# Order of the second layer's matmuls in the first feed-forward, and signals for the first constants of the next stage

## The chip, the cores and the metric

One core of a Trainium2 chip runs the whole program. The metric is the device time of one execution in microseconds (us). The engines are TensorE (PE in profile rows, its weight loads PEld), VectorE (DVE), ScalarE (ACT), GpSimd (POOL) and SyncE (SP), which here issues every transfer. Each engine runs its own list of instructions in order and meets the others through semaphores.

## The reference, cut to what matters

Two transformer layers work on 2048 tokens of width 512. Each layer adds an attention and a feed-forward, both fed by the same normalised input. The change touches the feed-forward of layer 0 and the start of the projections of layer 1:

```python
# layer 0, feed-forward: 16 blocks of 128 hidden units, 4 chosen for each token
h = jnp.einsum('nf,ibf->nib', xf, W1b)                      # first layer
h = jax.nn.gelu(h, approximate=False) * mask[:, :, None]
y = jnp.einsum('nib,fib->nf', h, W2b)                       # second layer
...
x = x + _L0_attn_ref(...) + _L0_ffn_ref(...)
xn = _layernorm(x, axis=-1)                                 # start of layer 1
k_r = hidden_states @ kr_w.T                                # hidden_states is xn
c_kv = hidden_states @ down_w.T
k_c = c_kv @ upk_w.T
v = c_kv @ upv_w.T
k = k * cos + _rotate_half(k) * sin
```

## The kernel before, in words

All products are made in three matmuls: each float32 operand is split into a high part and a low remainder, and `split_matmul` (L47 to L52) adds high by high, high by low and low by high into one bank of PSUM. A matmul with 512 moving columns is the unit of everything below.

`feed_forward0` goes through the 16 hidden blocks in four quarters (`NQ`), of four blocks each (`BPQ`). Within a quarter it goes through four chunks of 512 tokens (`NCH`), each of four tiles of 128 tokens (`TPC`). So there are 16 iterations. In one iteration:

- TensorE makes the first layer, 4 blocks of 12 matmuls, each into its bank `HB[b]`, and signals `hid`. Then it makes the second layer, another 48 matmuls, into the four banks `YB[t]`, one for each token tile.
- ScalarE takes a block through Gelu (`f_gl`, L919), and after the masking rounds it to the high part (`f_hT_hi`, L923). It makes the Gelu of block b before the high part of block b-1.
- VectorE multiplies the block by its mask (`f_h`, L1013, signal `masked`).
- GpSimd subtracts to make the low part (`f_hT_lo`, L940, signal `h_lo`). Only after `h_lo` may TensorE use the block in the second layer.
- VectorE adds the four finished `YB[t]` to the running sum `xacc` (L1025, signals `y_done` and `y_added`).
- Beside this, VectorE unpacks the 4-bit weights of layer 1's feed-forward, 21 operations in an iteration of quarters 1 and 2 and of the first three iterations of quarter 3 (L969 to L988), and splits the next quarter's weights in quarters 0 to 2 (ScalarE L905, VectorE L951).

The second layer is issued in two halves. The first waits for blocks 0 and 1 and makes, tile by tile, their six matmuls; the second waits for blocks 2 and 3 and does the same. `y_done` comes tile by tile in the second half.

`projections1` follows behind a barrier of all engines. SyncE issues the transfers: two weights, six constants (identity, epsilon and four rotation tables), two more weights, the first piece of the query weights, and the store of `xacc`. All six constants count on one signal, `c_in`. Meanwhile VectorE makes the statistics of the first 512 tokens (L1281, L1285); ScalarE takes the square root (L1232, needs epsilon), VectorE normalises (L1289, L1294), TensorE transposes (L1366, needs the identity), ScalarE and VectorE split the four weights (L1246, L1313) and the transposed chunk (L1237, L1300), and TensorE starts the key product (L50 to L52 on `k_wk`). The rotation tables are first used when VectorE multiplies that product (`k_rp`, L1325). ScalarE and TensorE each wait for the whole of `c_in` at the start of their list.

Of the kernel before, what the change touches and what calls it, by code (L numbers as in the profile page):

```python
# [14 lines left out]
P = 128  # L15
# [31 lines left out]
def split_matmul(pe, out, lhs, rhs, first, last, lsel, rsel):  # L47

    (lh, ll), (rh, rl) = lhs, rhs
    pe.matmul(out, lh[lsel], rh[rsel], start=first, stop=False)  # L50
    pe.matmul(out, lh[lsel], rl[rsel], start=False, stop=False)  # L51
    return pe.matmul(out, ll[lsel], rh[rsel], start=False, stop=last)  # L52
# [674 lines left out]
def feed_forward0(nc, ps, d, xacc):  # L727
# [3 lines left out]
    BPQ = NB // NQ  # L731
# [4 lines left out]
    with ExitStack() as ctx:  # L736
# [8 lines left out]
        w2 = [sb(f"w2_{s}", [P, 2, BPQ, C], F32R) for s in ("hi", "lo")]  # L745
# [4 lines left out]
        hT = [sb(f"hT_{s}", [P, BPQ, CH], F32R) for s in ("hi", "lo")]  # L750
# [40 lines left out]
        with nc.Block() as block:  # L791
# [235 lines left out]
            @block.tensor  # L1027
            def _(pe):
                for q in range(NQ):
                    p = q % 2  # L1030
                    with pe.Fori(0, NCH) as c:
                        it = c + q * NCH
                        if q == 0:
                            pe.wait_ge(xt_in.sem, xt_in.now(c, 32))

                        pe.wait_ge(w_lo.sem, (q + 1) * PRO if q else KC)
                        for b in range(BPQ):
                            pe.wait_ge(gelu.sem, gelu.before(it, b + 1))
                            for k in range(KC):
                                last = split_matmul(pe, HB[b], [w[:, p] for w in w1], xt, k == 0, k == KC - 1,  # L1040
                                                    np.s_[:, k, b * P:(b + 1) * P],
                                                    (slice(None), k, bass.ds(c * CH, CH)))
                            last.then_inc(hid.sem, 1)
                        if q == 0:
                            pe.wait_ge(w_lo.sem, PRO)
                        for bs in (range(BPQ - 2), range(BPQ - 2, BPQ)):
                            pe.wait_ge(h_lo.sem, h_lo.now(it, bs[-1] + 1))
                            for t in range(TPC):
                                if bs[0] == 0:
                                    pe.wait_ge(y_added.sem, y_added.before(it, t + 1))  # L1050
                                for b in bs:
                                    last = split_matmul(pe, YB[t], hT, [w[:, p] for w in w2], b == 0, b == BPQ - 1,
                                                        np.s_[:, b, t * P:(t + 1) * P], np.s_[:, b, :])
                                if bs[0] > 0:
                                    last.then_inc(y_done.sem, 1)


# [8 lines left out]
def projections1(nc, ps, d, xacc, xt):  # L1066

    with ExitStack() as ctx:
# [3 lines left out]
        def sig(name, per, credit=False):  # L1072
            return Signal(nc, ctx, "k1_" + name, per, credit)
# [28 lines left out]
        BANKS = [*XB, *MB]  # L1102

        apart = sig("apart", 0)
        c_in = sig("c_in", 0)
        w_in = [sig(f"w_in{i}", 0) for i in range(len(weights))]
        w_hi = sig("w_hi", 0)
        w_lo = sig("w_lo", 0)
# [23 lines left out]
        q_sum = sig("q_sum", 2 * NCH, credit=True)  # L1132
        q_stored = [sig(f"q_stored{i}", 32 * NCH // 2, credit=True) for i in range(2)]

        CONSTS = [(ident[:], d["c_ident"]), (eps[:], d["c_eps"]), (cosk[:], d["c_cosk"]), (sink[:], d["c_sink"]),
                  (cosq[:], d["c_cosq"]), (sinq[:], d["c_sinq"])]
        ALL_CONSTS = 16 * len(CONSTS)

        def staged(n):

            _, k, m = weights[n][0].shape
            room = (kq[:].rearrange("p t n -> p (t n)"), qo[:].rearrange("p a b n -> p (a b n)"))[n // 2]
            return room[:, (n % 2) * KC * R1:(n % 2) * KC * R1 + k * m].rearrange("p (k n) -> p k n", k=k)
# [4 lines left out]
        with nc.Block() as block:  # L1148
            @block.sync
            def _(sp):  # L1150
                for s in q_stored:
                    s.give_credit(sp)
                for n, name in enumerate(names[:2]):
                    sp.dma_start(staged(n), d[name].rearrange("(k p) n -> p k n", p=P)).then_inc(w_in[n].sem, 16)
                for dst, src in CONSTS:
                    sp.dma_start(dst, src).then_inc(c_in.sem, 16)
                for n, name in enumerate(names[2:], 2):
                    sp.dma_start(staged(n), d[name].rearrange("(k p) n -> p k n", p=P)).then_inc(w_in[n].sem, 16)

                def load_wq(g):  # L1160
                    sp.dma_start(wq_stage[:], d["WqT"][:, bass.ds(g * QW, QW)].rearrange("(k p) n -> p k n", p=P)
                                 ).then_inc(wq_in.sem, 16)

                load_wq(0)
                sp.dma_start(d["x2"], xacc[:]).then_inc(x_stored.sem, 16)
                for c in range(NCH):
                    sp.wait_ge(xt_lo.sem, xt_lo.now(c, KC))
                    for s in range(2):
                        sp.dma_start(d["xt"][s][:, :, c * CH:(c + 1) * CH],
                                     xt[s][:, :, c * CH:(c + 1) * CH].bitcast(F32)).then_inc(x_stored.sem, 16)  # L1170
                    for t, ready in ((0, rotated.now(c, 1)), (2, rotated.now(c, 2))):
                        sp.wait_ge(rotated.sem, ready)
                        sp.dma_start(d["KT"][t, :, c * CH:(c + 1) * CH], kq[:, t, :]).then_inc(k_stored.sem, 16)
                    for t, ready in ((1, kc_out.now(c, 1)), (3, kc_out.now(c, 2))):
                        sp.wait_ge(kc_out.sem, ready)
                        sp.dma_start(d["KT"][t, :, c * CH:(c + 1) * CH], kq[:, t, :]).then_inc(k_stored.sem, 16)
                    for t in range(TPC):
                        sp.wait_ge(v_out.sem, v_out.now(c, t + 1))
                        seq, tile = divmod(c * TPC + t, SEQ // P)
                        for r in range(4):  # L1180
                            sp.dma_start(d["V"].rearrange("g b p j e -> b j p g e")[seq, 4 * tile + r, :, :, :],
                                         vt[32 * r:32 * r + 32, t % 2, :].rearrange("p (g e) -> p g e", e=HD1)
                                         ).then_inc(v_stored[t % 2].sem, 16)

                def store_q(g, c):
                    for i in range(2):
                        sp.wait_ge(q_sum.sem, q_sum.now(g, 2 * c + i + 1))
                        sp.dma_start(d["QT"][bass.ds(g, 1), i, :, c * CH:(c + 1) * CH].squeeze(0), qo[:, c % 2, i, :]
                                     ).then_inc(q_stored[c % 2].sem, 16)

                with sp.Fori(0, NKV - 1) as g:
                    sp.wait_ge(wq_lo.sem, wq_lo.now(g, 1))
                    load_wq(g + 1)
                    for c in range(NCH):
                        store_q(g, c)
                for c in range(NCH):
                    store_q(NKV - 1, c)
                sp.wait_ge(x_stored.sem, 16 + 32 * NCH)
                sp.wait_ge(k_stored.sem, k_stored.now(NCH, 0))
                for s in v_stored:  # L1200
                    sp.wait_ge(s.sem, s.now(NCH, 0))
                for s in q_stored:
                    sp.wait_ge(s.sem, s.now(NKV, 0))
# [21 lines left out]

            @block.scalar
            def _(act):
                act.wait_ge(c_in.sem, ALL_CONSTS)

                def root(c):  # L1230
                    act.wait_ge(ln_chain.sem, ln_chain.now(c, 2 * TPC))
# [44 lines left out]
            def _(dve):  # L1276
# [20 lines left out]
                def split_turned(c):  # L1297
                    for k in range(KC):
                        dve.wait_ge(xt_hi.sem, xt_hi.now(c, k + 1))
                        nc.vector.tensor_tensor(xt[1][:, k, c * CH:(c + 1) * CH], XB[k],  # L1300
                                                xt[0][:, k, c * CH:(c + 1) * CH].bitcast(F32), ALU.subtract
                                                ).then_inc(xt_lo.sem, 1)
# [8 lines left out]
                for n, w in enumerate(weights):  # L1311
                    dve.wait_ge(w_hi.sem, n + 1)
                    nc.vector.tensor_tensor(w[1][:], staged(n), w[0][:].bitcast(F32), ALU.subtract  # L1313
                                            ).then_inc(w_lo.sem, 1)
                dve.wait_ge(c_in.sem, ALL_CONSTS)
                split_turned(0)
                for c in range(NCH):
                    if c + 1 < NCH:
                        dve.wait_ge(ln_chain.sem, ln_chain.now(c + 1, 0))
# [35 lines left out]
            @block.tensor  # L1355
            def _(pe):
                q_done.give_credit(pe)
                pe.wait_ge(c_in.sem, ALL_CONSTS)

                def turn(c):  # L1360
                    pe.wait_ge(ln_chain.sem, ln_chain.now(c + 1, 0))
# [851 lines left out]
```

## Time and profile before

| what | us |
|---|---|
| median of three runs (2312.14 to 2317.91) | 2313.44 |
| the profiled execution: its time | 2313.69 |
| its span, first to last instruction | 2311.9 |
| TensorE busy in the span | 2077.5 |
| VectorE busy | 1544.6 |
| ScalarE busy | 874.0 |
| GpSimd busy | 486.2 |
| the first feed-forward's matmuls, first to last start | 324.30 to 684.53 |
| first transposes of the projections | 700.60 |
| first matmul of the key product | 706.91 |

A timeline row reads: start, duration, engine, line, operation, what it writes and reads, count. What stands in brackets at its end is the idle time of the engine before it and who ended it. Matmuls overlap: a row's duration is its latency, and the distance of two starts is what one costs. A row of a stage gives, for each engine, busy time and number of instructions, then the granted TensorE clock as a share of full speed, the share of the transfer engines and GB/s.

### The profile page before, as it was taken

The numbers are of one execution on the slowest core, as the hardware profiler recorded it, in microseconds if no ns is written. First come the engines' busy times: TensorE is split into PE (matmuls) and PEld (weight loads), VectorE is DVE, ScalarE is ACT, GpSimd is POOL, SyncE is SP. The second block draws the span as 40 slices with busy tenths as digits, with TensorE's granted clock in tenths as the row PEclk, the third lists the DMA queues.
The fourth block names the chain that finished last, engine by engine and source line by source line (L and its number), as shares of the span: only waits on it lengthen the run. The fifth ranks groups of instructions, "written<-read, shape, count | busy, mean of one in ns | idle before, by whom it ended". The sixth has DMA issues, their size and how long they took to land. (4 is left out here: it accounts for less than half of the span.)

```text
span 2311.9 us, 54178 instructions
## 1 busy us (share of the span) xinstructions
PE 2077.5 (90%) x22192; PEld 1468.3 (64%) x22192; DVE 1544.6 (67%) x2534; ACT 874.0 (38%) x1836; POOL 486.2 (21%) x408
## 2 busy tenths in 40 slices
PE   7999969999988999778888888888888699999997
PEld 5777758877766788634444444444444588787776
DVE  6544423799966354478989988889998330477776
ACT  4222123222213200045655655565665221234443
POOL 0111112222310145401111111111111444221111
PEclk9999989999998999979999999999999899999999
DMA  5122154344326533333443333343332555320101
GB/s 179 56 93 75 38 195 151 109 134 132 121 94 250 177 121 121 110 77 84 102 106 99 93 100 87 84 113 107 92 92 77 214 170 183 111 90 19 55 1 37
DMA packets 197121, 251.26 MB, mean 109 GB/s; under 512 B 38496, under 2 KB 119712, under 8 KB 194208
## 3 DMA queue, kind: packets, MB, share of 16 engines
q1 hardware_dynamic: 196032, 247.85, 34.7%
q8 instruction: 166, 2.72, 0.5%
q14 instruction: 59, 0.48, 0.1%
q10 hardware_dynamic: 864, 0.21, 0.0%
HBM read 165.08 MB, written 82.90 MB: 107 GB/s over the span
## 5 line engine op out<-in xcount | busy, mean ns | idle before, releaser
L1614 ACT ACTIVATE a_prob<-ps,a_nmax 128x256 f32<-128x256 f32 (+7 forms) x512 | 377.4, 739 | 349.4 <-DVE a_nmax L1642 211.2
L1727 PE MATMUL ps<-a_kt,a_q 64*128 64x512 f32 (+5 forms) x1536 | 380.4, 536 | 85.3 <-ACT a_prob L1614 63.6
L1642 DVE TENSOR_REDUCE a_nmax<-ps 128x1 f32<-128x1024 f32 (+3 forms) x256 | 256.1, 1000 | 73.0 <-PE ps L1727 71.5
L1659 DVE STREAM_TRANSPOSE a_pt_long<-a_prob 128x512 f32<-128x512 f32 (+3 forms) x512 | 278.1, 580 | 0.0
L1727 PEld LDWEIGHTS ps<-a_kt,a_q 64*128 64x128 f32 x1536 | 143.1, 193 | 184.5 <-ACT a_prob L1614 116.7
L1741 PE MATMUL ps<-a_pt_long,a_v 32*64 32x256 f32 (+3 forms) x7808 | 228.6, 344 | 2.5 <-issue 1.0
L2021 DVE SCALAR_TENSOR_TENSOR f_part<-ps,f_gu_scale,f_part 128x512 f32<-128x512 f32 x264 | 184.6, 745 | 65.8 <-PE ps L2068 52.5
L1741 PEld LDWEIGHTS ps<-a_pt_long,a_v 32*64 32x64 f32 x7808 | 153.9, 132 | 105.1 <-issue 77.1
L1694 POOL TENSOR_TENSOR a_o<-a_left 128x256 f32<-128x256 f32 x128 | 90.3, 726 | 595.5 <-ACT a_left L1624 595.5
L940 POOL TENSOR_TENSOR f_hT_lo<-f_h,f_hT_hi 128x512 fp32r<-128x512 f32 x64 | 89.7, 1407 | 294.5 <-ACT f_hT_hi L923 294.5
L1724 PE MATMUL ps<-a_causal,a_identb 64*128 64x128 bf16 x1024 | 112.2, 224 | 39.5 <-ACT a_prob L1614 39.5
L1645 DVE TENSOR_REDUCE a_nmax<-ps 128x2 f32<-128x1024 f32 (+3 forms) x128 | 104.8, 819 | 37.7 <-PE ps L1727 37.3
L919 ACT ACTIVATE f_gl<-ps 128x512 f32<-128x512 f32 x64 | 38.3, 599 | 225.0 <-PE ps L52 225.0
L50 PE MATMUL ps<-f_xt_hi,f_w_hi 128*128 x256 | 100.4, 392 | 17.8 <-DMA f_xt_lo<-scratch_xt 17.8
L50 PE MATMUL ps<-o_wo_hi,o_oT_hi 128*128 128x512 f32 x256 | 100.4, 392 | 15.8 <-POOL o_oT_lo L1844 15.8
L1659 DVE STREAM_TRANSPOSE a_pt_short<-a_prob 128x512 f32<-128x512 f32 (+3 forms) x256 | 114.2, 484 | 0.0
L1724 PEld LDWEIGHTS ps<-a_causal,a_identb 64*128 64x128 bf16 x1024 | 45.7, 95 | 104.8 <-issue 78.1
L2010 POOL TENSOR_TENSOR f_hT_lo<-f_h,f_hT_hi 128x512 fp32r<-128x512 f32 x44 | 57.5, 1306 | 254.9 <-ACT f_hT_hi L1966 254.9
L1223 POOL TENSOR_TENSOR k_qo<-k_rp 128x512 f32<-128x512 f32 x64 | 87.4, 1387 | 102.5 <-DVE k_rp L1346 102.5
L1741 PEld LDWEIGHTS ps<-a_pt_short,a_v 32*64 32x64 f32 x3712 | 65.9, 132 | 67.5 <-issue 67.4
L50 PE MATMUL ps<-f_w_hi,f_hT_hi 128*128 128x512 f32 x256 | 101.3, 396 | 6.4 <-POOL f_hT_lo L940 6.4
L1346 DVE TENSOR_TENSOR k_rp<-ps,k_cosq 128x512 f32<-128x512 f32 x64 | 43.9, 685 | 94.1 <-POOL k_qo L1223 81.2
(228 smaller groups left out, 4552.4 us busy)
## 6 DMA issues: line engine op xcount, KB each, us to landing
a_q<-scratch_QT SPq DMA_DIRECT2D x512, 64.0 KB, 2.1
scratch_QT<-k_qo SPq DMA_DIRECT2D x64, 256.0 KB, 2.3
a_v<-scratch_V SPq DMA_DIRECT2D x64, 256.0 KB, 4.3
scratch_OT<-a_o SPq DMA_DIRECT2D x32, 512.0 KB, 3.4
o_of<-scratch_OT SPq DMA_DIRECT2D x32, 512.0 KB, 4.1
f_block<-in_packed SPq DMA_DIRECT2D x33, 256.0 KB, 3.4
f_mask<-scratch_maskT SPq DMA_DIRECT2D x16, 512.0 KB, 5.1
a_kt<-scratch_KT SPq DMA_DIRECT2D x128, 64.0 KB, 4.2
```

Source lines behind the costliest of these rows:

```text
L50: pe.matmul(out, lh[lsel], rh[rsel], start=first, stop=False)
L940: nc.gpsimd.tensor_tensor(hT[1][:, b, :], h[:, b % 2, :], hT[0][:, b, :].bitcast(F32), ALU.subtract).then_inc(h_lo.sem, 1)
L1223: nc.gpsimd.tensor_tensor(qo[:, c % 2, i, :], rp[:, 2 * i, :], rp[:, 2 * i + 1, :], op).then_inc(q_sum.sem, 1)
L1614: last = nc.scalar.activation(prob[:, n % PRING, s].rearrange("p (a w) -> p a w", w=w), SC[n % 2][:, a, 0:w], ACT.Exp, bias=nmax[:, n % 4, ...
L1642: nc.vector.tensor_reduce(nmax[:, n % 4, 0:1], SC[n % 2][:, :, 0:width(0, t)], AX.XY, ALU.max, negate=True).then_inc(maxed, 1)
L1645: nc.vector.tensor_reduce(nmax[:, n % 4, :], SC[n % 2][:, :, 0:width(1, t)], AX.X, ALU.max, negate=True).then_inc(maxed, 1)
L1659: last = nc.vector.transpose(pt[hf][:, lo:hi, h, t - FIRST[hf], :], src.rearrange("p (j k) -> p j k", k=32))
L1694: nc.gpsimd.tensor_tensor(o[:, :, :, i, :], left[:, i, 0], left[:, i, 1], ALU.mult).then_inc(o_done, 1)
L1724: pe.matmul(sc[:, a, w - P:w], identb[r, s, :], causal[r, s, :], start=s == 0, stop=False, skip_group_check=True)
L1727: last = pe.matmul(sc[:, a, 0:w], q[r, slot, heads[a * hf], :], kt[r, b, keys], start=not masked, stop=True, skip_group_check=True)
L1741: last = pe.matmul(out[:, :, a - t0:4, :], v[rows, b, j, :], pt[hf][rows, j, c::2, a - t0:4, :], start=j == 0, stop=j == BLOCKS[hf] - 1, s ...
L2021: nc.vector.scalar_tensor_tensor(part[:, s % 2, i, :], PB[(2 * k + i) % 4], gu_scale[:, s % NBK, i, k:k + 1], part[:, s % 2, i, :], ALU.mu ...
```

## The change

The second layer of the first feed-forward is issued in four parts instead of two: one block at a time, over all four token tiles, each part behind its own wait for `h_lo`. The matmuls and their number are the same. In the projections, epsilon and the identity get a signal of their own, `first_in`, and are issued first; the four weights follow, and the four rotation tables come behind them. ScalarE and TensorE wait for `first_in` alone. VectorE waits for the tables after it has split the first transposed chunk.

```diff
-                        for bs in (range(BPQ - 2), range(BPQ - 2, BPQ)):
-                            pe.wait_ge(h_lo.sem, h_lo.now(it, bs[-1] + 1))
+                        for b in range(BPQ):
+                            pe.wait_ge(h_lo.sem, h_lo.now(it, b + 1))
                             for t in range(TPC):
-                                if bs[0] == 0:
+                                if b == 0:
                                     pe.wait_ge(y_added.sem, y_added.before(it, t + 1))
-                                for b in bs:
-                                    last = split_matmul(pe, YB[t], hT, [w[:, p] for w in w2], b == 0, b == BPQ - 1,
-                                                        np.s_[:, b, t * P:(t + 1) * P], np.s_[:, b, :])
-                                if bs[0] > 0:
+                                last = split_matmul(pe, YB[t], hT, [w[:, p] for w in w2], b == 0, b == BPQ - 1,
+                                                    np.s_[:, b, t * P:(t + 1) * P], np.s_[:, b, :])
+                                if b == BPQ - 1:
                                     last.then_inc(y_done.sem, 1)
...
-        c_in = sig("c_in", 0)
+        first_in, c_in = sig("first_in", 0), sig("c_in", 0)
...
-        CONSTS = [(ident[:], d["c_ident"]), (eps[:], d["c_eps"]), (cosk[:], d["c_cosk"]), (sink[:], d["c_sink"]),
-                  (cosq[:], d["c_cosq"]), (sinq[:], d["c_sinq"])]
+        CONSTS = [(cosk[:], d["c_cosk"]), (sink[:], d["c_sink"]), (cosq[:], d["c_cosq"]), (sinq[:], d["c_sinq"])]
...
-                for n, name in enumerate(names[:2]):
+                sp.dma_start(eps[:], d["c_eps"]).then_inc(first_in.sem, 16)
+                sp.dma_start(ident[:], d["c_ident"]).then_inc(first_in.sem, 16)
+                for n, name in enumerate(names):
                     sp.dma_start(staged(n), d[name].rearrange("(k p) n -> p k n", p=P)).then_inc(w_in[n].sem, 16)
                 for dst, src in CONSTS:
                     sp.dma_start(dst, src).then_inc(c_in.sem, 16)
-                for n, name in enumerate(names[2:], 2):
-                    sp.dma_start(staged(n), d[name].rearrange("(k p) n -> p k n", p=P)).then_inc(w_in[n].sem, 16)
...
             def _(act):
-                act.wait_ge(c_in.sem, ALL_CONSTS)
+                act.wait_ge(first_in.sem, 32)
...
             def _(dve):
...
+                split_turned(0)
                 dve.wait_ge(c_in.sem, ALL_CONSTS)
-                split_turned(0)
...
             def _(pe):
                 q_done.give_credit(pe)
-                pe.wait_ge(c_in.sem, ALL_CONSTS)
+                pe.wait_ge(first_in.sem, 32)
```

## Rows read from the trace of the kernel before

**Rows 1.** Busy time by engine in seven iterations of quarters 1 and 2.
```profile
436.00:596.00 160.00, 154.49 (x674) 125.65 (x674) 145.66 (x217) 40.78 (x70) 40.49 (x28) 1.00 0.43 132
```

**Rows 2.** Timeline of TensorE where the second layer starts, quarters 0 and 3.
```profile
402.65 0.39 PE L52 MATMUL ps<-f_xt_hi,f_w_lo 128*128 x1
403.03 0.47 PE L50 MATMUL ps<-f_w_hi,f_hT_hi 128*128 128x512 f32 x1
...
606.38 0.39 PE L51 MATMUL ps<-f_xt_lo,f_w_hi 128*128 x1
606.61 0.39 PE L52 MATMUL ps<-f_xt_hi,f_w_lo 128*128 x1
607.86 0.50 PE L50 MATMUL ps<-f_w_hi,f_hT_hi 128*128 128x512 f32 x1 [0.86 <-POOL f_hT_lo L940]
```

**Rows 3.** Waits of VectorE in the same 160 us: total, times, longest.
```profile
DVE f_w_lo L951 <- ACT f_w_hi L905: 9.5, 7, 1.4
```

**Rows 4.** Timeline of VectorE: first maskings of two iterations, and two unpacking steps.
```profile
601.87 0.68 DVE L1013 TENSOR_TENSOR f_h<-f_gl,f_mask 128x512 f32<-128x512 f32 x1
...
606.60 1.76 DVE L980 SCALAR_TENSOR_TENSOR f_block<-f_mag,f_block 128x512 f32<-128x512 f32 x1
608.39 1.68 DVE L982 TENSOR_TENSOR f_block<-f_block,f_sign 128x512 int32<-128x512 int32 x1
...
622.59 0.68 DVE L1013 TENSOR_TENSOR f_h<-f_gl,f_mask 128x512 f32<-128x512 f32 x1
```

**Rows 5.** Timeline of GpSimd: low part of block 1, then of blocks 1, 2 and 3.
```profile
401.55 1.38 POOL L940 TENSOR_TENSOR f_hT_lo<-f_h,f_hT_hi 128x512 fp32r<-128x512 f32 x1 [1.43 <-ACT f_hT_hi L923]
...
606.03 1.78 POOL L940 TENSOR_TENSOR f_hT_lo<-f_h,f_hT_hi 128x512 fp32r<-128x512 f32 x1 [1.30 <-ACT f_hT_hi L923]
608.23 1.29 POOL L940 TENSOR_TENSOR f_hT_lo<-f_h,f_hT_hi 128x512 fp32r<-128x512 f32 x1 [0.43 <-ACT f_hT_hi L923]
611.42 1.32 POOL L940 TENSOR_TENSOR f_hT_lo<-f_h,f_hT_hi 128x512 fp32r<-128x512 f32 x1 [1.90 <-ACT f_hT_hi L923]
```

**Rows 6.** Timeline where two of GpSimd's subtractions stand back to back.
```profile
653.13 3.10 POOL L940 TENSOR_TENSOR f_hT_lo<-f_h,f_hT_hi 128x512 fp32r<-128x512 f32 x2 [1.35 <-ACT f_hT_hi L923]
...
653.57 1.52 DVE L969 TENSOR_SCALAR f_sign<-f_block,f_up_shift 128x512 int32<-128x512 int32 x1
```

**Rows 7.** Timeline of VectorE at the start of the projections.
```profile
698.32 0.18 DVE L1289 RECIPROCAL k_rstd<-k_std 128x4 f32<-128x4 f32 x1 [9.46 <-ACT k_std L1232]
...
714.02 0.69 DVE L1325 TENSOR_TENSOR k_rp<-ps,k_cosk 128x512 f32<-128x512 f32 x1 [4.47 <-PE ps L52]
```

**Rows 8.** Timeline of ScalarE at the start of the projections.
```profile
688.95 1.28 ACT L1232 ACT_TABLE_LOAD   x1 [13.03 <-DVE k_mv L1285]
697.99 0.30 ACT L1232 ACTIVATE k_std<-k_mv,k_eps 128x4 f32<-128x4 f32 x1 [7.76 <-DMA k_sinq<-in_c_sinq]
...
700.62 1.04 ACT L1246 ACTIVATE k_wuv_hi<-k_qo 128x1024 fp32r<-128x1024 f32 x1
```

**Rows 9.** Timeline of TensorE: the start of the key product.
```profile
706.91 0.80 PE L50 MATMUL ps<-xt_hi,k_wk_hi 128*128 128x512 f32 x1 [2.66 <-DVE xt_lo L1300]
```

**Rows 10.** Transfers issued between 680 and 800 us: count, KB, issue to landing.
```profile
scratch_V<-k_vt SPq DMA_DIRECT2D x64, 64.0 KB, 1.9
...
k_cosk<-in_c_cosk SPq DMA_DIRECT2D x1, 512.0 KB, 6.0
...
k_qo<-in_wuvT SPq DMA_DIRECT2D x1, 512.0 KB, 9.6
...
k_eps<-in_c_eps SPq DMA_DIRECT2D x1, 0.5 KB, 4.6
```

**Rows 11.** Timeline of SyncE: first, fifth and tenth transfer of the projections.
```profile
686.07 0.39 SPq L1154 DMA_DIRECT2D k_kq<-in_wkT  x1
...
688.07 0.43 SPq L1156 DMA_DIRECT2D k_cosk<-in_c_cosk  x1
...
690.45 0.96 SPq L1158 DMA_DIRECT2D k_qo<-in_wuvT  x1
```

## The prediction

> **What bounds the kernel now.** I read the busy time by stage first, then the waits of each engine in the stage that the change touches, then the timelines at the points of the waits.
>
> The second and third quarters of the feed-forward hold two engines near their limit: in seven iterations (160 us) TensorE is busy 154.5 us and VectorE 145.7 us [rows 1]. The question is which one waits for the other. In those 160 us VectorE has one kind of wait only, for the high part of the split weights, 9.5 us in seven pieces of 1.4 us [rows 3]. That wait hangs on its own last masking and not on TensorE. Busy time and this wait make 155.2 of the 160 us; the rest is small gaps between dependent unpacking steps. So VectorE never waits for a matmul there: it is the bound, at 160/7 = 22.9 us for an iteration. TensorE needs less. Its starts are 0.227 us apart (606.38 and 606.61 [rows 2]), so 96 matmuls take 21.8 us, and the rest is a stall at the start of each second layer: 607.86 - 606.61 - 0.23 = 1.02 us [rows 2], released by the low part of block 1, ready at 606.03 + 1.78 = 607.81 [rows 4 and 5]. There are eight such stalls, one in each of eight iterations (447.33 is the first, 607.86 the last).
>
> Where VectorE has room (quarter 0, the first iteration of quarter 1, and quarter 3 behind its first iteration), TensorE is the bound. Even there the second layer starts late: 403.03 against 402.65 + 0.23 = 402.88 [rows 2]. The low part of block 1 is ready only at 401.55 + 1.38 = 402.93 [rows 5]. The matmul behind it starts 0.31 us later instead of 0.23.
>
> Between the last matmul of the feed-forward (684.53) and the key product (706.91 [rows 9]) TensorE does only 16 transposes. The chain there runs: square root, normalising, weight splits, transposed chunk, key product. The square root starts at 697.99, released by the last rotation table [rows 8], though it needs none of them; its table load began at 688.95, when the statistics were done, and ended at 690.23 [rows 8].
>
> **The feed-forward's part.** Let S be the start of the second layer. Before, it needs block 1 at S and block 3 at S + 24 x 0.227 = S + 5.44. After, blocks 0, 1, 2, 3 are needed at S, S + 2.72, S + 5.44, S + 8.16. No need comes earlier. The instructions are the same; two more semaphore waits stand in front of matmuls whose queue holds work, and I count them at nothing, because the mid-layer wait of the kernel before leaves no gap above 0.245 us in any iteration. If each cost the 0.24 us that the late one costs, three a layer over 16 iterations would be 11.5 us, the upper end.
>
> *TensorE-bound iterations.* Block 1 gets 2.7 us of air, and block 0 is ready one block earlier. What goes is 0.15 + 0.08 = 0.23 us in each: four in quarter 0, 0.2 in the first of quarter 1: 0.9 + 0.2; and three in quarter 3, 0.5 together. VectorE's additions move: `y_done` of the first tile comes 2.04 us later and the four come 0.68 us apart instead of 1.36. An addition is issued about every 0.6 us, so the last one ends where it did, and the next masking comes more than 2 us later. That cover hides it.
>
> *VectorE-bound iterations.* Here removing the stall gives nothing for each iteration. VectorE's list is not shortened, so the period stays 22.9 us, and TensorE's spare 1.1 us turns up as waits elsewhere (mostly in front of block 1's part). What it gives is a phase: TensorE may run further ahead of VectorE. In the last such iteration the blocks are ready at 604.73, 607.81, 608.23 + 1.29 = 609.52 and 611.42 + 1.32 = 612.74 [rows 5] (the first is 603.30 + 1.43, block 0 on the same engine). The effective start is the largest of 604.73, 607.81 - 2.72 = 605.09, 609.52 - 5.44 = 604.08 and 612.74 - 8.16 = 604.58. That is 605.09 instead of 607.81: 2.72 us, once, not eight times. The advance is kept in quarter 3, as VectorE has no split there: its first masking comes 622.59 - 601.87 = 20.7 us after the one before [rows 4], less than TensorE's 21.8.
>
> VectorE's own timeline moves forward by quarter 0's 0.9 us, since its first masking of quarter 1 hangs on TensorE. Sum: 0.9 + 2.7 + 0.6 (quarter 3, and part of quarter 1's) = 4.2 us.
>
> *The unknown in it.* With TensorE ahead, the Gelu of block 3 comes earlier on ScalarE and no longer stands before the high part of block 2. GpSimd's third subtraction then can start right behind the second, at 607.82 instead of 608.23 [rows 5]. VectorE's L980 waits there already: it started at 606.60, took 1.76 us, and L982 behind it took 1.68 us [rows 4]; both take 0.69 us where GpSimd is idle. So each of GpSimd's subtractions holds one VectorE operation for about 1 us. Where two subtractions stand back to back (3.10 us for both), the waiting VectorE operation gets in between: it ends at 653.57 + 1.52 = 655.09, and the second subtraction lies behind [rows 6]. By that the order stays: L980, then the third subtraction, then L982, and the price is nothing. If GpSimd goes first instead, L980 ends 1.3 us later and L982 finds the way free: 0.37 us an iteration, eight times 3.0 us. If L982 gains, as a third subtraction that ends sooner would let it, it is up to 0.3 us an iteration, 2.4 us of gain. I take nothing, by the nearest row.
>
> The Trainium skill (SBUF — State Buffer, "Who interferes with whom") says that a VectorE instruction with two SBUF inputs and a GpSimd instruction that reads SBUF exclude each other, and that issue order decides who blocks. The 1.76 us of L980 [rows 4] agrees. By that rule L980, issued 1.2 us before the third subtraction is, goes first: the sum would be the same 4.2 us.
>
> **The projections' part** (times as if the feed-forward ended where it does). After the change the square root needs epsilon, the transposes the identity. They are the first two transfers, issued at 686.07 and some 0.45 us later [rows 11]. From below such a transfer lands in 1.9 us, from above in the 4.6 us that epsilon took behind 1 MB [rows 10]: 688.0 to 690.7. The table load ends at 690.23, so the wait costs 0 to 0.5 us; I take 0, since nothing large stands before it. The square root moves from 697.99 to 690.25: 7.74 us. From there VectorE is busy without a gap up to the last low part of the transposed chunk (reciprocal at 698.32 [rows 7], key product 706.91), so the chain is 8.6 us long and moves as a whole, if its other inputs come in time.
>
> The other inputs are the weights. VectorE needs the high part of the fourth weight by 695.5 (its split of it began at 703.24, less 7.74), so ScalarE must start its 1.04 us [rows 8] at 694.4. Before, 1.6 MB had landed when the first table did, at 688.07 + 6.0 = 694.1 [rows 10, 11]. After, the fourth weight ends at 1.9 MB. At 1.3 us for 0.5 MB that is 694.8; without epsilon's dip in the flow it could be 694.1. So it is late by 0 to 1 us; I take 0.4. All the tables have landed when the fourth weight had before: 690.45 + 9.6 = 700.05 [rows 10, 11]. VectorE comes to that wait at about 699.5, and behind it stand 2.9 us of statistics; they are wanted only once the key product is there, at 714.02 - 7.3 = 706.7 [rows 7]. Room of 3.7 us: the tables' later place costs nothing.
>
> The transfer queue carries the same bytes, so the store of `xacc` lands when it did, about 711; the first values are stored near 719, behind it. From the key product on, all shifts as a whole. Gain 7.3 us, 6.2 to 7.8.
>
> The granted clock is 0.50, the lower level (1.2 GHz), from 689.3 on, 4.5 us after the last matmul, and comes back at 709.7, when the key product has run 2.8 us. Afterwards TensorE's pause is 8.3 us instead of 16; the fall still lies inside it, and the first seven matmuls of the key product should again cost 0.43 us instead of 0.23. The Trainium skill (TensorE: Matmul & The Clock Gate, "What's actually happening") calls the watch on activity free-running. By that rule the return can shift against the matmuls and the count of slow ones can vary. The other sum would be better or worse by up to about 1.4 us, seven matmuls.
>
> **Sum.** 4.2 + 7.3 = 11.5 us. The profiled execution took 2313.69 (span 2311.9), so it would take 2302.2; the median of the runs shown, 2313.44, is 0.25 below it, so 2301.9.
>
> **Rivals.**
> - *GpSimd takes the turn* (above): the feed-forward gives back 3.0 us, 2304.9. For it: the two subtractions would touch with no gap at all. Against it: [rows 6].
> - *The feed-forward gives nothing*: the satisfied waits in mid-layer cost as much as is won, 2313.4 - 7.3 = 2306.1. For it: the change doubles them. Against it: the one of today leaves no gap.
> - *All eight stalls go*, each iteration falling to 21.8 us: the stalls are 0.4 and seven times 1.03 us, 7.6 in all, and the late starts of the other eight iterations 1.7: 7.6 + 1.7 + 7.3 = 16.6, so 2296.8. Against it: VectorE's full 22.9 us [rows 1 and 3].
> - *The constants were not the wait*: weights or epsilon release the square root and the splits as late as before, and only the 4.2 us are left, 2309.2, no change that can be told. For it: ScalarE's splits followed the square root at once, so their transfers' own times don't show. Against it: the landing times [rows 10].
> - *Slower*: VectorE is the bound in eight iterations, and a new meeting with GpSimd there counts eight times. Were two more VectorE operations an iteration held for 1.1 us each, that is 17.6 us, 2319.5. It decides the sign from 11.5/8 = 1.4 us an iteration on. Against it: GpSimd still has four subtractions an iteration, and today each already holds one operation.
>
> **How the numbers follow.** Chances: the forecast 0.62, GpSimd's turn 0.13, nothing from the feed-forward 0.10, all stalls 0.03, the constants 0.08, slower 0.04. Three runs of this kernel can tell about 0.3%, 6.9 us, from no change. The first four cases are faster by more: 0.88. The constants' case is the same, 0.08; slower 0.04. Range: upwards to the second rival, 2306.1; downwards the forecast with 2.4 us from L982 and 0.5 us from the projections, 2299.0. That leaves out 0.15 in named cases.
>
> **What would show it.** Right: in quarters 1 and 2 VectorE's first maskings still 22.9 us apart; TensorE waiting about 1 us an iteration, now at block 1's part; second layers of quarter 0 exactly 0.23 us behind the first; last matmul of the feed-forward near 680.3; table load and square root adjoining; the key product near 695.4, 11.5 us earlier than 706.91; 2.0 us or more of idle VectorE before `k_rp`. Wrong: a period of VectorE other than 22.9 us, ScalarE waiting for `in_wuvT`, VectorE waiting for `in_c_sinq` in front of `k_rp`, or slow matmuls in larger number.

## The result, and the profile after

| | before | after |
|---|---|---|
| median of five runs each, us | 2313.18 | 2301.69 |
| lowest to highest | 2311.39 to 2317.91 | 2299.28 to 2306.12 |
| span of the profiled execution | 2311.9 | 2298.5 |

The ratio of after to before is 0.9945, with a 95% interval of 0.993 to 0.996: faster by 11.5 us. The forecast was 2301.9, range 2299.0 to 2306.1.

The spans differ by 13.4 us, and 2.5 us of that lie ahead of the change: the first matmul of the feed-forward starts at 324.30 before and at 321.81 after, behind code that is the same in both. So I compare distances inside the stages:

| distance, us | before | after | gain | forecast |
|---|---|---|---|---|
| feed-forward, first to last matmul start | 360.23 (324.30 to 684.53) | 355.90 (321.81 to 677.71) | 4.33 | 4.2 |
| last matmul to key product | 22.38 (to 706.91) | 15.58 (to 693.29) | 6.80 | 7.3 |
| key product to first rotation | 7.11 (to 714.02) | 7.39 (to 700.68) | -0.28 | 0 |
| from there to the end of the span | 1597.9 | 1597.9 | 0.0 | 0 |

**The feed-forward.** The same 160 us of quarters 1 and 2, busy time by engine. It answers to [rows 1].

```profile
436.00:596.00 160.00, 157.75 (x685) 127.55 (x684) 145.64 (x218) 41.11 (x71) 43.43 (x28) 1.00 0.44 132
```

VectorE's busy time is the same to 0.02 us. TensorE has 11 matmuls more in the window: it runs ahead of VectorE, but not at a better rate. VectorE's only waits there answer to [rows 3] and have not moved:

```profile
DVE f_w_lo L951 <- ACT f_w_hi L905: 9.5, 7, 1.4
```

VectorE's timeline, the first maskings of two iterations and the two unpacking steps of [rows 4]:

```profile
575.44 0.68 DVE L1013 TENSOR_TENSOR f_h<-f_gl,f_mask 128x512 f32<-128x512 f32 x1
...
598.36 0.68 DVE L1013 TENSOR_TENSOR f_h<-f_gl,f_mask 128x512 f32<-128x512 f32 x1
...
603.08 1.79 DVE L980 SCALAR_TENSOR_TENSOR f_block<-f_mag,f_block 128x512 f32<-128x512 f32 x1
604.90 1.66 DVE L982 TENSOR_TENSOR f_block<-f_block,f_sign 128x512 int32<-128x512 int32 x1
606.48 0.68 DVE L1013 TENSOR_TENSOR f_h<-f_gl,f_mask 128x512 f32<-128x512 f32 x1
```

The period is 598.36 - 575.44 = 22.92 us, as before. TensorE's starts answer to [rows 2]:

```profile
399.37 0.39 PE L52 MATMUL ps<-f_xt_hi,f_w_lo 128*128 x1
399.59 0.39 PE L50 MATMUL ps<-f_w_hi,f_hT_hi 128*128 128x512 f32 x1
...
600.39 0.39 PE L52 MATMUL ps<-f_xt_hi,f_w_lo 128*128 x1
601.26 0.50 PE L50 MATMUL ps<-f_w_hi,f_hT_hi 128*128 128x512 f32 x1 [0.49 <-POOL f_hT_lo L940]
...
603.89 0.39 PE L52 MATMUL ps<-f_w_hi,f_hT_lo 128*128 128x512 f32 x1
604.37 0.50 PE L50 MATMUL ps<-f_w_hi,f_hT_hi 128*128 128x512 f32 x1
```

In quarter 0 the second layer follows at 0.22 us: the late start is gone. In the iteration at 600 us there is a stall of 0.87 - 0.23 = 0.64 us before block 0's part and one of 0.48 - 0.23 = 0.25 us before block 1's. With the slow second start behind each they make the 1.1 us that TensorE has to spare. They begin in the iteration at 486.64 us; before, the stalls began at 447.33.

GpSimd answers to [rows 5]:

```profile
599.79 1.42 POOL L940 TENSOR_TENSOR f_hT_lo<-f_h,f_hT_hi 128x512 fp32r<-128x512 f32 x1 [13.51 <-ACT f_hT_hi L923]
602.51 3.50 POOL L940 TENSOR_TENSOR f_hT_lo<-f_h,f_hT_hi 128x512 fp32r<-128x512 f32 x2 [1.30 <-ACT f_hT_hi L923]
```

The second and third subtraction now touch. L980 still ends at 603.08 + 1.79 = 604.87, long before the pair ends at 606.01.

**The projections.** ScalarE and VectorE, answering to [rows 8] and [rows 7]:

```profile
682.13 1.28 ACT L1230 ACT_TABLE_LOAD   x1 [12.88 <-DVE k_mv L1283]
683.43 0.30 ACT L1230 ACTIVATE k_std<-k_mv,k_eps 128x4 f32<-128x4 f32 x1
684.03 1.06 ACT L1244 ACTIVATE k_wk_hi<-k_kq 128x1024 fp32r<-128x1024 f32 x1 [0.30 <-DMA k_kq<-in_wkT]
...
688.52 1.06 ACT L1244 ACTIVATE k_wuv_hi<-k_qo 128x1024 fp32r<-128x1024 f32 x1 [1.05 <-DMA k_qo<-in_wuvT]
```

```profile
689.61 1.23 DVE L1311 TENSOR_TENSOR k_wuv_lo<-k_qo,k_wuv_hi 128x1024 fp32r<-128x1024 f32 x1 [0.85 <-ACT k_wuv_hi L1244]
690.76 2.48 DVE L1298 TENSOR_TENSOR xt_lo<-ps,xt_hi 128x512 fp32r<-128x512 f32 x4
693.70 2.47 DVE L1279 BATCH_NORM_STATS2 k_stats<-xacc 128x6 f32<-128x512 f32 x4 [0.47 <-DMA k_sinq<-in_c_sinq]
...
700.68 0.69 DVE L1323 TENSOR_TENSOR k_rp<-ps,k_cosk 128x512 f32<-128x512 f32 x1 [4.18 <-PE ps L52]
```

The square root adjoins its table load. The fourth weight is late and costs VectorE 0.85 us. The tables are late by 0.47 us, which disappears in the 4.18 us that VectorE waits for the key product. The transfers, issue to landing, answering to [rows 10]:

```profile
k_qo<-in_wuvT SPq DMA_DIRECT2D x1, 512.0 KB, 6.8
...
k_sinq<-in_c_sinq SPq DMA_DIRECT2D x1, 512.0 KB, 9.9
...
k_ident<-in_c_ident SPq DMA_DIRECT2D x1, 64.0 KB, 1.8
k_eps<-in_c_eps SPq DMA_DIRECT2D x1, 0.5 KB, 2.0
```

### The profile page after: what moved, and what is told of

Same layout as the page of the kernel before. It is cut to its first block and busy times, and to the rows that moved or that the text cites. A ratio compares the mean times of both kernels' runs of the same rounds, so it can differ in the third digit from the quotient of the medians.

```text
span 2298.5 us, 54178 instructions
## 1 busy us (share of the span) xinstructions
PE 2076.8 (90%) x22192; PEld 1470.2 (64%) x22192; DVE 1543.5 (67%) x2534; ACT 873.2 (38%) x1836; POOL 490.5 (21%) x408
## 5 line engine op out<-in xcount | busy, mean ns | idle before, releaser
L1739 PE MATMUL ps<-a_pt_short,a_v 32*64 32x192 f32 (+3 forms) x3712 | 102.6, 304 | 2.5 <-ACT a_left L1622 2.3
```

Source lines behind the costliest of these rows:

```text
L1739: last = pe.matmul(out[:, :, a - t0:4, :], v[rows, b, j, :], pt[hf][rows, j, c::2, a - t0:4, :], start=j == 0, stop=j == BLOCKS[hf] - 1, s ...
```

## The experiments

"Key product" is the distance from the last matmul of the feed-forward to the first of the key product; "feed-forward" is that from its first matmul to its last. Both are of one profile each; medians and ratios are of the timed runs, against runs of the kernel before on the same chip. The first four share their runs of before, as do the next three and the last three.

| run | feed-forward | key product | median (before) | ratio, 95% |
|---|---|---|---|---|
| e1, order only | 356.54 | 24.39 | 2310.8 (2314.5) | 0.9985, 0.9976 to 0.9993 |
| e2, signals only | 360.24 | 15.45 | 2308.34 (2314.5) | 0.9974, 0.9965 to 0.9983 |
| e3, shorter list, before | 353.16 | 22.57 | 2306.91 (2314.5) | 0.9969, 0.9959 to 0.998 |
| e4, shorter list, after | 349.63 | 16.42 | 2296.33 (2314.5) | 0.9923, 0.9911 to 0.9936 |
| e5, one and three | 376.90 | 22.25 | 2332.36 (2315.61) | 1.008, 1.0062 to 1.0097 |
| e6, tables first | 355.90 | 20.59 | 2309.94 (2315.61) | 0.9977, 0.9967 to 0.9987 |
| e7, chunk first | 356.51 | 13.38 | 2299.6 (2315.61) | 0.9936, 0.9921 to 0.9951 |
| e8, wait filled, before | 353.34 | 24.45 | 2306.28 (2314.26) | 0.9962, 0.995 to 0.9974 |
| e9, wait filled, after | 349.70 | 16.51 | 2297.86 (2314.26) | 0.9922, 0.9909 to 0.9936 |
| e10, both | 349.59 | 13.37 | 2293.86 (2314.26) | 0.9905, 0.9891 to 0.9919 |

### e1 and e2: each part of the change alone

The edits are the two halves of the diff.

> Only the second layer's new order, the projections as before. My theory: the feed-forward, first to last matmul start, falls from 360.2 us to 355.9 (0.23 us in each of eight iterations bound by TensorE, and one phase of 2.7 us), the distance from the last matmul to the key product stays 22.4 us; time 2308.9, within 0.3 per cent of before. Rival, all of the gain comes from the constants: feed-forward 360.2, time 2313.2. Rival, all stalls go: feed-forward 351, time 2304.

> Only the projections' signals and the order of their transfers, the feed-forward as before. My theory: the two parts add up. Feed-forward 360.2 us, distance from the last matmul to the key product 15.6 us instead of 22.4, time about 2306.4. Rival, the two parts overlap (the store of the running sum and the stores behind it eat part of it): the time is nearer to 2310.

The new order alone is worth 3.7 us by the medians (0.9985). In its profile the feed-forward takes 356.54 us; 0.6 us of the difference to 355.90 stand at its start, where the first matmuls run at the lower clock: the first second layer starts 13.06 us after the first matmul, against 12.50. The signals alone are worth 6.2 us (0.9974), and the key product comes at 15.45. Together they have 9.9 us by the medians, where the whole change has 11.5; that is inside the intervals, and no loss between the two can be seen. The 24.39 us of e1 is unlike the 22.38 before, in code that is the same. The last table landed 2 us later after its issue than in the profile of before (8.5 us there):

```profile
k_sinq<-in_c_sinq SPq DMA_DIRECT2D x1, 512.0 KB, 10.5
```

It is 10.5 us in e8 too, with 24.45. So the wait that the change removes is 2 us longer in some executions. In the five profiles with the old signals (before, e1, e3, e5, e8) the key product comes 22.25 to 24.45 us after the last matmul, in the four with the new ones and the old place of the chunk (after, e2, e4, e9) 15.45 to 16.51, where the fourth weight lands 6.7 to 7.8 us after its issue. The 6.8 us are those of one pair of profiles.

### e3 and e4: a shorter list for VectorE

The last two of every six unpacking operations are made on 128 of 512 columns, which leaves the other columns of those weights unfinished.

```diff
-  done = nc.vector.scalar_tensor_tensor(pk, mag[:], 64.0, pk, ALU.mult, ALU.min)
+  done = nc.vector.scalar_tensor_tensor(pk[:, :P], mag[:, :P], 64.0, pk[:, :P], ALU.mult, ALU.min)
...
-  done = nc.vector.tensor_tensor(pk32, pk32, sign32, ALU.bitwise_or)
+  done = nc.vector.tensor_tensor(pk32[:, :P], pk32[:, :P], sign32[:, :P], ALU.bitwise_or)
```

> The kernel before, with the last two of every six unpacking operations on VectorE made on 128 of 512 columns (the rest of the weights of layer 1's feed-forward stays unfinished, so the output is not the reference's). It shortens VectorE's list by about 2 us in an iteration that unpacks. My theory, VectorE is the bound there: the eight stalls of TensorE go, the iterations of quarters 1 and 2 fall from 22.9 to 22.0 us, feed-forward 352.6, time 2305.6. Rival, GpSimd's subtractions or the chain through one block set the period: it stays at 22.9.

> The changed kernel with the same shortening of VectorE's list (the same part of the computation left out). My theory: the changed order left VectorE's 22.9 us an iteration as they were, so now they fall to TensorE's 21.8; feed-forward from 355.9 to about 350, time 2295.7. Rival, the new order has already taken all that was to be had in the feed-forward: 2301.7, as the changed kernel.

The same 160 us, first of e3 and then of e4:

```profile
436.00:596.00 160.00, 160.00 (x701) 130.66 (x700) 132.64 (x226) 41.09 (x73) 37.43 (x29) 1.00 0.45 138
```

```profile
436.00:596.00 160.00, 160.00 (x707) 132.48 (x707) 133.80 (x227) 42.23 (x75) 38.38 (x30) 1.00 0.45 139
```

TensorE is now busy all the time in both, and VectorE waits for Gelu (in e4 11.7 us in 23 pieces; in the changed kernel it had no such wait):

```profile
DVE f_h L1013 <- ACT f_gl L919: 11.7, 23, 0.9
```

The second layers of e3 stand 21.99 us apart, those of e4 21.76. So VectorE's list was the bound in both orders, and the new order had left this untaken: e4 gains another 6.3 us in the feed-forward (355.90 to 349.63). The 0.23 us between the two periods is the late start, now seen alone in iterations that all belong to TensorE.

### e5: an early first wait with a bad order behind it

```diff
-  for bs in (range(BPQ - 2), range(BPQ - 2, BPQ)):
+  for bs in (range(1), range(1, BPQ)):
```

> The kernel before, with the second layer in two halves of one and three blocks instead of two and two: block 0 alone over the four tiles, then blocks 1 to 3 tile by tile. The first wait is as early as in the changed kernel, but block 3 is needed 2.7 us after the start instead of 8.2. My theory, when each block is needed is all that counts: block 3 is ready 4.0 us after the first layer's end, so TensorE stalls 1.3 us in each of the eight iterations that it bounds (23.2 us each), and the phase towards VectorE in the other eight gets 2.2 us worse; feed-forward 372, time about 2325. Rival, the gain of the changed kernel comes from the earlier first wait: 2309.

The rival is refuted: 1.008 instead of less than 1. The size was off: 376.9 us where 372 were expected. TensorE and GpSimd of e5 in quarter 2:

```profile
568.53 0.39 PE L52 MATMUL ps<-f_xt_hi,f_w_lo 128*128 x1
568.76 0.39 PE L50 MATMUL ps<-f_w_hi,f_hT_hi 128*128 128x512 f32 x1
...
573.11 0.50 PE L50 MATMUL ps<-f_w_hi,f_hT_hi 128*128 128x512 f32 x1 [1.46 <-POOL f_hT_lo L940]
```

```profile
570.16 2.90 POOL L940 TENSOR_TENSOR f_hT_lo<-f_h,f_hT_hi 128x512 fp32r<-128x512 f32 x2 [1.35 <-ACT f_hT_hi L923]
```

Block 3 is ready at 573.06, 4.3 us behind the first layer, not 4.0. I had taken the 4.0 from a quarter without unpacking on VectorE. The period is 23.24 us in quarter 0, as expected, but 23.5 in quarters 1 and 2, where I had expected VectorE's 22.9: here the chain through block 3 is longer than VectorE's list, and VectorE waits for Gelu. Most of the missing 5 us lie there. From the second layer at 451.10 to that at 639.51, the eight iterations that VectorE had bounded, e5 takes 188.4 us, 5.9 more than the kernel before (447.33 to 629.85), where I had added 2.2. In quarter 3, whose first three iterations unpack too, the next two periods are 23.7 us and not 23.2, which is 1.0 us more.

### e6: the separate signal without the new order of transfers

The four tables are issued between the second and the third weight, as before; all else is the changed kernel.

> The changed kernel with its own signal for epsilon and identity, but the four rotation tables issued ahead of the third and fourth weight, as before. My theory: the fourth weight then lands as late as before, ScalarE waits for it with everything behind it, and the key product comes 4.6 us later than in the changed kernel (20.2 us after the last matmul of the feed-forward); time 2306.3. Rival, the separate signal is the whole gain and the order of the transfers is free: 15.6 us, 2301.7.

The key product comes at 20.59 us, 5.0 later than in the changed kernel. ScalarE shows why:

```profile
693.91 0.63 ACT L1246 ACTIVATE k_wuk_hi<-k_qo 128x512 fp32r<-128x512 f32 x1 [4.81 <-DMA k_qo<-in_wukT]
695.65 1.06 ACT L1246 ACTIVATE k_wuv_hi<-k_qo 128x1024 fp32r<-128x1024 f32 x1 [1.10 <-DMA k_qo<-in_wuvT]
```

Of the 6.8 us of this part the signal alone has 1.8; 5.0 need the order of the transfers too. As the distance before scatters by 2 us between profiles, the 1.8 is rough. The new order of the transfers without the separate signal was not run.

### e7: the chunk behind the first weight

```diff
                 for n, w in enumerate(weights):
                     act.wait_ge(w_in[n].sem, 16)
                     nc.scalar.activation(w[0][:], staged(n), ACT.Copy).then_inc(w_hi.sem, 1)
-                turned(0)
+                    if n == 0:
+                        turned(0)
```

and on VectorE likewise with `split_turned(0)`.

> The changed kernel, with ScalarE and VectorE taking the transposed chunk right behind the first weight and the other three weights after it, since the key product needs the first weight and the chunk alone. My theory: the wait for the fourth weight (1.05 us of ScalarE, 0.85 us of VectorE) and 3 us of splits leave the chain; it is then bound by the transposes; the key product comes 2.2 us earlier than in the changed kernel (13.4 us after the last matmul of the feed-forward), time 2299.5. Rival, the time is given back, since the second weight's split or the statistics of the next chunk come late: 2301.7.

The key product comes at 13.38 us, 2.2 earlier. The bound now is the chain through TensorE's transposes, the splits of their results and the key product:

```profile
688.24 3.65 PE L1366 MATMUL ps<-k_ident,k_xn 128*128 128x128 f32 x16 [7.93 <-DVE k_xn L1293]
693.30 0.80 PE L50 MATMUL ps<-xt_hi,k_wk_hi 128*128 128x512 f32 x1 [1.41 <-DVE xt_lo L1299]
```

The median is 2299.6, and the ratio 0.9936; its interval overlaps that of the changed kernel, so the distance in the profile shows the gain, and the time alone would not.

### e8 to e10: the wait of VectorE filled

With VectorE as the bound, its 1.37 us wait for the high part of the split weights is worth removing. The edit moves three unpacking operations into it:

```diff
+                        unpack_some(range(2 * BPQ - 2, 2 * BPQ + 1))
                         if q + 1 < NQ:
                             split((q + 1) % 2, c, c + (KC + q * NCH))
                         if q == 0:
                             dve.wait_ge(x_in.sem, x_in.now(c, 16))
-                        unpack_some(range(2 * BPQ - 2, OPS))
+                        unpack_some(range(2 * BPQ + 1, OPS))
```

> The kernel before, with three of VectorE's unpacking operations (1.5 us) moved ahead of the weight split in each iteration of quarters 1 and 2, into the 1.37 us in which VectorE waits there for ScalarE. All work is done. My theory, VectorE is the bound at 22.9 us: the period falls by the wait to 21.55, under TensorE's 22.0 with its late starts, so the stalls go; feed-forward 353, time about 2306. Rival, the operations are longer there since GpSimd's fourth subtraction runs beside them: period 22.5 or more, feed-forward 357.

> The changed kernel with the same move. My theory: period 21.8 us, TensorE's, in all 16 iterations, feed-forward 349.7 instead of 355.9, time 2295.5. Rival as for the same move in the kernel before: feed-forward 353 or more, time 2299 or more.

> Both further changes on top of the changed kernel: the unpacking moved ahead of the split, and the transposed chunk taken behind the first weight. My theory, they add up: feed-forward 349.7, key product 13.4 us after the last matmul, time 2293.3. Rival: one takes from the other, 2296.

In e8 the second layers of quarters 1 and 2 stand 22.0 us apart, TensorE's own pace with its late starts, and the feed-forward takes 353.34 us, where 353 were expected. The same 160 us of e9:

```profile
436.00:596.00 160.00, 160.00 (x708) 132.48 (x707) 155.25 (x228) 42.16 (x75) 45.96 (x30) 1.00 0.45 138
```

The second layers of e9 stand 21.76 us apart in all quarters, and its feed-forward takes the 349.70 us that were expected. VectorE does all its work and has no wait left in this stretch that the profile names. e10 has the lowest median of this study: 2293.86 us, ratio 0.9905, that is 20.4 us under before, where the change studied has 11.5, and its interval lies wholly below that of the change.

## Why the prediction was right

**The sum, and some luck in it.** Inside the stages the two profiles differ by 4.33 + 6.80 - 0.28 = 10.85 us, where 11.5 were forecast. That the medians differ by 11.5 and lie 0.2 us from the forecast is luck: the interval of the ratio allows a gain of 9 to 16 us. Two of the signs that I had named for being wrong did show, ScalarE waiting for `in_wuvT` (1.05 us) and VectorE for `in_c_sinq` (0.47 us); neither touches the mechanism, and what they cost is told below.

**VectorE is the bound in quarters 1 and 2, and the stall there is not a gain to be had eight times.** Shown: its period stayed 22.92 us, TensorE still stalls, and shortening (e4) or filling (e9) VectorE's list brings the 6.2 to 6.3 us that the new order left.

**One phase of 2.7 us.** Right in place and size. From VectorE's first masking to TensorE's second layer it was 607.86 - 601.87 = 5.99 us, and is 601.26 - 598.36 = 2.90; less the 0.36 us that TensorE now loses at block 1's part (the stall of 0.25 and the slow start of 0.11 behind it), that is a shift of 2.73 us, once. The sum of 4.2 measured 4.33. Where TensorE's spare time turned up was told wrongly: "mostly in front of block 1's part". The start is bound by block 0 (604.73 in the working) almost as tightly as by block 1 (605.09), so 0.64 us stand before block 0's part and 0.25 before block 1's.

**0.23 us in each iteration of TensorE.** Right: 0.37 to 0.38 us became 0.22, and e3 beside e4 shows it alone (21.99 and 21.76 us apart). The two further waits cost nothing: quarter 0's second layers have no gap.

**GpSimd's turn.** Right by the row on which it stood: GpSimd's two subtractions touch, L980 gets in between, and the fourth masking comes 8.12 us after the first (606.48 - 598.36), against 8.13. The Trainium skill (SBUF — State Buffer, "Who interferes with whom") has it that issue order decides who blocks; the trace agrees, with L980 issued at 603.08, ahead of the third subtraction, and done at 604.87, 1.14 us before the pair ends.

**The wait for six constants, though two are needed.** Right. Epsilon and identity landed in 2.0 and 1.8 us, and the square root has no wait. e6 adds that the signal without the order of the transfers brings only 1.8 of the 6.8 us.

**The fourth weight.** The step that was mis-sized: I took 0.4 us, it cost 0.85. It landed 9.2 us after the first issue (681.69 + 6.8 - 679.25) where I had reckoned 8.7. That is 0.45 of the 0.5 us by which the projections' part fell short; e7 takes it off the chain.

**The tables' later place costs nothing.** Right: 0.47 us of wait stand ahead of 4.18 us of idle time.

**The clock.** The sum held nearly (0.28 us off), the picture did not. I had the clock at its lower level from 4.5 us after the last matmul until the key product had run 2.8 us. The stages of the changed kernel, ending in granted clock, share of the transfer engines and GB/s:

```profile
683.00:684.00 1.00, 0.00 (x0) 0.00 (x0) 0.20 (x2) 0.71 (x2) 0.00 (x0) 0.69 1.06 367
...
690.00:693.30 3.30, 0.01 (x1) 0.02 (x1) 3.23 (x5) 1.52 (x4) 0.00 (x0) 0.97 1.02 399
...
694.00:696.00 2.00, 2.00 (x6) 1.60 (x5) 2.00 (x4) 0.00 (x0) 0.00 (x0) 0.50 0.95 401
```

It fell within 683 to 684, about 5.7 us behind the start of the last matmul (4.8 in the kernel before). It was back behind the transposes at 690, in a pause, fell again just as the key product began, and came back near 697. In other profiles it stayed low through e7's transposes and was up all through e10's key product. So the distance from the start of the key product to that of the next product is 5.58 us in e10, 6.90 in e2 and 8.43 in e3, where 24 matmuls at the higher clock take 5.44. Against the 6.91 us of before, these distances are 1.3 us less to 1.5 us more, about the 1.4 us either way that I had allowed. The Trainium skill (TensorE: Matmul & The Clock Gate, "What's actually happening") calls the watch free-running, and by that rule the same matmuls can meet either level; the trace agrees.

## What to carry to other kernels

When two engines look equally busy, ask which one has waits that hang on the other. Making the other engine's needs later removes its stalls only once, as a phase (a shift of one engine against the other, and not a gain in each iteration); the period changes when the bound engine's list gets shorter or a wait inside it is filled. And a signal that counts several transfers is as late as the last of them: give the first needed transfers their own, and put them and what stands behind them ahead in the queue. Here the signal without the order brought 1.8 of 6.8 us.

## What the runs showed of the hardware

- The granted clock fell 2.4 to 5.7 us behind the start of the last matmul of the feed-forward (e6 and the changed kernel), after the same matmuls. In several profiles (the changed kernel, e2, e4, e6, e9) it rose about when the 16 transposes ended (0.3 us before their end in e2, 0.2 to 0.7 us after it in the others), and it was low again when the key product began or 0.3 us later.
- Eight transfers in one queue, 3.1 MB up to and with the last table, landed that table 8.4 to 8.7 us after its issue in three profiles (before, e3, e5) and 10.5 us in two others of the same code (e1 and e8). e1 and e3 ran on the same chip. The cause stays open. The Trainium skill (DMA: Bandwidth & Descriptors, "Anatomy of one DMA — SWDGE (gpsimd) path") gives some 2 us as the fixed cost of a transfer that GpSimd issues. These are issued by SyncE, and the small ones in front land in much the same time, 1.8 to 2.0 us.
- One GpSimd subtraction of 128x512 holds one VectorE operation that is issued while it runs for about 1.1 us, also a short one: at 128 columns L980 takes 0.29 us alone and 1.37 us beside it (e4). It need not have two SBUF inputs: L975, with one, takes 0.43 us alone and 1.53 beside it. Narrowing an operation that stands there saves none of the hold.

```profile
506.17 1.53 DVE L975 TENSOR_SCALAR f_mag<-f_mag 128x512 int32<-128x512 int32 x1
...
508.99 1.37 DVE L980 SCALAR_TENSOR_TENSOR f_block<-f_mag,f_block 128x128 f32<-128x128 f32 x1
...
517.22 0.29 DVE L980 SCALAR_TENSOR_TENSOR f_block<-f_mag,f_block 128x128 f32<-128x128 f32 x1
```
